# Four self attentions of a decoder: turns woven into the value products of the half batch behind, and no unread products

## The chip, the cores and the metric

The kernel runs on one core of one Trainium2 chip. The metric is the device time of one execution in microseconds (us). The names of the engines are PE (TensorE, the matrix products), PEld (its weight loads), DVE (VectorE), ACT (ScalarE), POOL (GpSimd) and SP (SyncE, which issues transfers).

## The reference

A decoder of four layers works on x, 16 batches of 100 tokens with 128 features. Each layer has a self attention, a cross attention and a feed forward block. The change is in the self attentions alone. They have 16 heads of 8 features each. Layer 0 (`sa0` in the kernel), cut to its core:

```python
scores = jnp.einsum('bhqd,bhkd->bhqk', q, k) * scale
scores = jnp.where(causal[None, None], scores, -jnp.inf)
probs = jax.nn.softmax(scores / TEMP, axis=-1)
probs = probs * gate
out = jnp.einsum('bhqk,bhkd->bhqd', probs, v)
return (out @ w_out.T + b_out) * 0.1
```

Layers 1 and 3 (`sa1`, `sa3`) have the same form: `sa1` has no biases and quantised weights, `sa3` has normed queries and keys and biases. Layer 2 (`sa2`) is a differential attention without a causal mask: two softmax maps for each head, values of 16 features, and a root-mean-square norm of each head's output before the last product.

```python
att = att1 - lam * att2
y = jnp.einsum('bhts,bhse->bhte', att, v)
y = y * jax.lax.rsqrt(jnp.mean(y * y, axis=-1, keepdims=True) + RMS_EPS) * subln_w
```

## The kernel before

Each engine has its own program, written out by hand, and the engines meet at semaphores. The order of each engine's work is the order of its loops in the code; no planner moves anything.

A self attention first makes queries and keys, splits them, and lays them out through DRAM. Then comes its main loop, which is what the change touches. The loop goes over units (`all_units`): 4 units in `sa0`, `sa1` and `sa3` (`nsm` = 1, 4 batches in a unit), 8 units in `sa2` (`nsm` = 2, 2 batches in a unit, two maps). A unit has 8 steps `k`, and a step is a half batch: 8 heads, in two groups `c` of 4. So the loops have 32, 32, 64 and 32 steps. For one half batch:

- PE: `scores(k)` makes the scores, 100 rows by 2 x 400 columns; in the causal layers each group is two products (the mask, then the scores). The results lie in banks 0 and 1 or 2 and 3, by the parity of `k`.
- DVE: `shift(k)` takes the row maxima (L1732) and subtracts them in place (L1733), and signals `shifted`.
- ACT: the exponential (L1188) of all 800 columns into `probs`, and signals `probs_ready`.
- PE: `turn(k)` transposes the 8 maps by products with the identity: 8 products of float32, which show as 16 records in the trace (L2652). Each group signals `turned`.
- ACT: two copies (L1200) bring the turned maps from PSUM into `probsT`, and signal `probsT_ready`.
- PE: `values(k)` multiplies the turned maps with the values: 8 products, 16 records (L2668), each with a full set of 100 x 100 weights and only 9 columns (17 in `sa2`). The last column counts the sum of the probabilities. Two half batches fill bank 7, and the second signals `o_full`.
- DVE: `normalise` divides by that sum (L1742, then L1745 or L1749) and gives bank 7 back with `o_free`. There is one such bank.

PE interleaves these over three half batches: in step k it does the four unread products, the turns of k, the scores of k + 2 and the value products of k - 1. The unread products (`unread`, L2640) are four products of 400 columns whose results nobody reads. Further, at set steps of a unit, PE makes the value rows of the next unit (`value_rows`, L2617 for the bias where there is one, and L2618), the transposes of the finished output of the unit before (`features`, L2681) and the last product (`project`, L2690). In `sa2`, DVE's `finish` and ACT's `root` work out the norm of the outputs (L1757 to L1764).

## Time and profile before

| | |
|---|---|
| median of 3 runs | 6178.4 us (6163.06 to 6204.71) |
| the profiled execution's own time | 6208.25 us |
| its span, first to last instruction | 6206.5 us |
| mean granted TensorE clock over the span | 0.818 of full speed |
| PE busy | 4731.2 us (76%) |
| DVE busy | 3437.1 us (55%) |
| ACT busy | 2441.8 us (39%) |
| main loops of the four self attentions, first to last row maxima | 161.2, 134.1, 345.4 and 161.9 us |

Busy shares are averages over stages with different limits, so a stage has to be read by itself. A full clock of 1.00 is 2.4 GHz, 0.50 is 1.2 GHz; a mean in between is a mixture of stretches at these two levels. A product of PE and the weight load of the next one overlap, and the end of a product is modelled, so the start of a record and the start of the next one tell more than a duration.

### The profile page before, as it was taken

The page shows a single profiled execution, that of the slowest core. Times are in us where ns is not written, and L with a number is a line of the kernel's source. Part 1 is how long each engine was busy: PE and PEld are TensorE (multiplying, and loading weights), DVE is VectorE, ACT ScalarE, POOL GpSimd, SP SyncE. Part 2 cuts the span into 40 slices and gives each one's busy share as a digit, 9 for nine tenths or more (in the row PEclk, how much of TensorE's full clock was granted, in tenths as well). Part 3 has the DMA queues.
Part 4 walks back from the last instruction along what each step waited for, and adds up shares of the span by engine and source line. Part 5 has one row for each costly group of instructions (what it writes and reads, how often), then busy time and mean ns, then how long its engine had stood idle before and what let it go on. Part 6 is the DMA issues. An engine that isn't in the chain of part 4 may idle for free. (4 is left out here: it accounts for less than half of the span.)

```text
span 6206.5 us, 84643 instructions
## 1 busy us (share of the span) xinstructions
PE 4731.2 (76%) x22582; PEld 3354.9 (54%) x22582; DVE 3437.1 (55%) x5067; ACT 2441.8 (39%) x3674; POOL 1999.7 (32%) x1091
## 2 busy tenths in 40 slices
PE   7999999999798866669878888888486444432698
PEld 6778778888544755348845555555274222221344
DVE  3444444444345422444556666664646999987444
ACT  2345555555222311123335555554123555540122
POOL 0055555555100000000036666664001555550000
PEclk7789999999799965687779999998677666655699
DMA  2100000000011312121111112110020000000011
GB/s 74 48 8 16 16 16 16 16 16 8 13 42 29 70 36 58 41 82 31 28 43 43 42 42 46 43 38 20 11 43 20 22 21 21 21 16 0 5 46 38
DMA packets 153375, 193.27 MB, mean 31 GB/s; under 512 B 91760, under 2 KB 136576, under 8 KB 152864
## 3 DMA queue, kind: packets, MB, share of 16 engines
q1 hardware_dynamic: 152992, 188.87, 12.5%
q8 instruction: 154, 2.52, 0.2%
q14 instruction: 229, 1.88, 0.1%
HBM read 134.07 MB, written 19.05 MB: 25 GB/s over the span
## 5 line engine op out<-in xcount | busy, mean ns | idle before, releaser
L1021 POOL TENSOR_TENSOR pexp_lo<-arena,pexp_hi 128x800 fp32r<-128x800 f32 x384 | 727.8, 1895 | 413.8 <-POOLq L1020 413.8
L976 POOL TENSOR_TENSOR pexp_lo<-arena,pexp_hi 128x800 fp32r<-128x800 f32 x384 | 628.4, 1636 | 515.6 <-POOLq L975 515.6
L1947 DVE TENSOR_REDUCE arena<-ps 128x1 f32<-128x482 f32 (+3 forms) x624 | 393.3, 657 | 404.1 <-DVEq L1925 388.9
L2092 DVE TENSOR_REDUCE arena<-ps 100x1 f32<-100x482 f32 (+1 forms) x768 | 476.6, 656 | 219.0 <-DVEq L2061 200.7
L1282 ACT ACTIVATE arena<-ps 128x800 f32<-128x800 f32 x384 | 322.3, 839 | 554.1 <-ACTq L1280 552.2
L1348 ACT ACTIVATE arena<-ps 128x800 f32<-128x800 f32 x384 | 321.7, 838 | 402.2 <-ACTq L1342 396.8
L2399 DVE MATCH_REPLACE8 arena<-arena 100x1444 f32<-100x1444 f32 x256 | 423.0, 1673 | 0.0
L3022 PE MATMUL ps<-kst,qs 96*100 96x482 f32 (+1 forms) x768 | 334.0, 436 | 116.4 <-PEq L2982 112.5
L1732 DVE TENSOR_REDUCE arena<-ps 100x8 f32<-100x800 f32 x160 | 158.7, 992 | 392.1 <-DVEq L1729 392.1
L3260 PE MATMUL ps<-arena,chunk 128*128 128x400 f32 x648 | 286.3, 524 | 72.6 <-PEq L3259 72.5
L2652 PE MATMUL ps<-w_const,arena 100*100 100x100 f32 x2560 | 311.2, 287 | 37.9 <-PEq L2648 37.9
L2652 PEld LDWEIGHTS ps<-w_const,arena 100*100 100x100 f32 x2560 | 309.6, 201 | 53.4 <-issue 42.9
L3164 PE MATMUL ps<-w_const,w_cross 100*128 100x100 f32 x192 | 43.2, 381 | 382.2 <-PEq L3161 382.2
L1283 ACT ACTIVATE pexp_hi<-ps 128x800 fp32r<-128x800 f32 x384 | 319.4, 832 | 0.0
L1349 ACT ACTIVATE pexp_hi<-ps 128x800 fp32r<-128x800 f32 x384 | 319.4, 832 | 0.0
L2389 DVE MAX8 arena<-arena 100x8 f32<-100x1444 f32 x192 | 311.5, 1677 | 0.0
L2489 DVE TENSOR_TENSOR arena<-ps,arena 128x400 f32<-128x400 f32 x256 | 147.0, 574 | 292.1 <-DVEq L2480 183.5
L1200 ACT ACTIVATE arena<-ps 100x400 f32<-100x400 f32 x320 | 160.5, 504 | 372.4 <-ACTq L1199 372.4
L1060 POOL TENSOR_TENSOR arena<-arena 100x1444 f32<-100x1444 f32 x64 | 207.8, 3246 | 285.9 <-POOLq L1059 285.9
L1524 ACT ACTIVATE arena<-ps 128x400 f32<-128x400 f32 x256 | 129.1, 504 | 423.6 <-ACTq L1521 423.4
L2914 PE MATMUL ps<-pexp_hi,ctxk_hi 128*97 128x400 f32 (+1 forms) x768 | 283.3, 369 | 15.1 <-PEq L2909 12.8
L921 POOL MEMSET k_diag<- 96x6400 f32 x4 | 21.7, 5428 | 833.2 <-POOLq L920 833.2
(358 smaller groups left out, 11004.8 us busy)
## 6 DMA issues: line engine op xcount, KB each, us to landing
ctxT<-in_ctxT SPq DMA_DIRECT2D x64, 541.5 KB
ctxk<-in_ctx SPq DMA_DIRECT2D x48, 528.0 KB
kst<-mid SPq DMA_DIRECT2D x128, 180.5 KB, 3.1
heads_dram<-arena SPq DMA_DIRECT2D x20, 800.0 KB
chunk<-in_ff_chunks SPq DMA_DIRECT2D x77, 193.0 KB, 2.4
arena<-gate_dram SPq DMA_DIRECT2D x64, 200.0 KB, 3.1
kst<-xn SPq DMA_DIRECT2D x64, 180.5 KB, 2.9
q_rows<-heads_dram SPq DMA_DIRECT2D x36, 200.0 KB
```

The lines of the kernel that those rows point to most:

```text
L976: own(nc.gpsimd.tensor_tensor(pexp_lo[p % 3][:, :, :], pexp[p % 3], pexp_hi[p % 3][:, :, :], ALU.subtract))
L1021: own(nc.gpsimd.tensor_tensor(pexp2_lo[p % 3][:, :, :], pexp2[p % 3], pexp2_hi[p % 3][:, :, :], ALU.subtract))
L1282: nc.scalar.activation(pexp[p % 3], of, ACT.Exp, scale=scale).then_inc(s.pexp_ready, 1)
L1283: own(nc.scalar.activation(pexp_hi[p % 3][:, :, :], of, ACT.Exp, scale=scale))
L1348: nc.scalar.activation(pexp2[p % 3], of, ACT.Exp, scale=scale).then_inc(s.pexp_ready, 1)
L1349: own(nc.scalar.activation(pexp2_hi[p % 3][:, :, :], of, ACT.Exp, scale=scale))
L1947: peak = nc.vector.tensor_reduce(mparts[0:at.stop - at.start, m, c:c + 1], bank(k, z - a, at.stop - at.start), AX.X, ALU.max)
L2092: peak = nc.vector.tensor_reduce(mparts2[:, h, c:c + 1], bank(k, z - a, S), AX.X, ALU.max)
L2389: nc.vector.max(tops[:, k, at], left[k]).then_inc(done[i], 1)
L2399: nc.vector.match_replace(left[k], tops[:, k, at], scores_sb[i] if r == 0 else left[k], TAKEN).then_inc(done[i], 1)
L2652: last = mm(bank(4 + c, S, S, j * S), probs[:, k % 2, at:at + S], ident[0:S, 0:S], start=True, stop=True)
L3022: ins = mm(bank(k, z - a, S), qs[par][0:C, g, S * (h % 4):S * (h % 4) + S], kst[0:C, g, a:z], start=True, stop=True)
```

## The change

On PE a step now has another order. It waits for the exponentials of k first, makes the scores of k + 2, and then goes through the 8 heads: one turn of half batch k, one value product of half batch k - 1, and so on. The waits for bank 7 (`o_free`) and for the values (`v_ready`) stand ahead of the first turn, and the wait for the turned maps of the half batch behind is taken group by group. The function `unread` and its calls are gone. In `sa2`, the two `features` move from steps 3 and 4 to 4 and 5 and `project` from 5 to 6; in the others they stay.

On ACT the exponential of k + 1 now comes before the copies of the turned maps of k; one exponential stands ahead of the loop.

On DVE, `finish` is cut in two: the squares and their sums stay at step 2, and the rest, which waits for ACT's root, is called at step `nsm` + 1 (3 in `sa2`, 2 in the others, where it only signals).

```diff
-    TURNS_AT = {1: (3,), 2: (3, 4)}
+    TURNS_AT = {1: (3,), 2: (4, 5)}
+    PROJECT_AT = {1: 5, 2: 6}
...
+            def exponential(k):
+                act.wait_ge(s.shifted, 1)
+                act.sem_inc(s.shifted, -1)
+                nc.scalar.activation(probs[:, k % 2, :].rearrange("p (c t) -> p c t", c=2),
+                                     ps[0:S, 2 * (k % 2):2 * (k % 2) + 2, 0:GT], ACT.Exp,
+                                     scale=float(cfg["scale"])).then_inc(s.probs_ready, 1)
...
             def unit(u, par, first=False, last=False):
                 for k in range(8):
...
+                    if k < 7 or not last:
+                        exponential((k + 1) % 8)
...
                     if not first and k == 2:
+                        squared_sums(1 - par)
+                    if not first and k == nsm + 1:
                         finish(1 - par)
...
-            def unread(n):
-
-                for i in range(n):
-                    mm(bank(4 + i % 2, GT, S), ident_bf[0:S, 0:S], causal_bf[:, :], start=True, stop=True)
-
-            def turn(k, first):
-                if not first:
-                    pe.wait_ge(s.probsT_ready, 2)
-                    pe.sem_inc(s.probsT_ready, -2)
-                unread(4)
-                pe.wait_ge(s.probs_ready, 1)
-                pe.sem_inc(s.probs_ready, -1)
...
+            def turns(k, behind, par):
+
+                if behind is not None:
+                    values_wait(behind)
                 for c in range(2):
+                    if behind is not None:
+                        pe.wait_ge(s.probsT_ready, 1)
+                        pe.sem_inc(s.probsT_ready, -1)
                     for j in range(4):
+                        at = c * GT + j * S
+                        ins = mm(bank(4 + c, S, S, j * S), probs[:, k % 2, at:at + S], ident[0:S, 0:S], start=True, stop=True)
+                        if j == 3:
+                            ins.then_inc(s.turned, 1)
+                        if behind is not None:
+                            value(behind, par, c, j)
...
             def unit(u, par, first=False, last=False):
                 for k in range(8):
-                    turn(k, first and k == 0)
+                    pe.wait_ge(s.probs_ready, 1)
+                    pe.sem_inc(s.probs_ready, -1)
                     if k < 6:
                         scores(k + 2, par)
                     elif not last:
                         scores(k - 6, 1 - par)
                     if k > 0:
-                        values(k - 1, par)
-                    elif not first:
-                        values(7, 1 - par)
+                        turns(k, k - 1, par)
+                    else:
+                        turns(0, None if first else 7, 1 - par)
```

The PE program at the second step (k = 1) of the first unit of `sa0`, before (unread products, turns, scores, value products, value rows):

```order
L2640 MATMUL ps<-causal_bf,ident_bf 100x400 [waits probsT_ready]
L2640 MATMUL ps<-causal_bf,ident_bf 100x400 x3
L2652 MATMUL ps<-w_const,arena 100x100 [waits probs_ready]
L2652 MATMUL ps<-w_const,arena 100x100 x7
L2633 MATMUL ps<-causal_bf,ident_bf 100x400
L2634 MATMUL ps<-k_diag_51,q_rows_49 100x400
L2633 MATMUL ps<-causal_bf,ident_bf 100x400
L2634 MATMUL ps<-k_diag_51,q_rows_49 100x400
L2668 MATMUL ps<-arena 100x9 [waits o_free,v_ready]
L2668 MATMUL ps<-arena 100x9 x7
```

The same step of the change, up to the turn that waits for the second group (L2645 and L2646 are the scores, L2678 a turn, L2663 a value product):

```order
L2645 MATMUL ps<-causal_bf,ident_bf 100x400 [waits probs_ready]
L2646 MATMUL ps<-k_diag_51,q_rows_49 100x400
L2645 MATMUL ps<-causal_bf,ident_bf 100x400
L2646 MATMUL ps<-k_diag_51,q_rows_49 100x400
L2678 MATMUL ps<-w_const,arena 100x100 [waits o_free,v_ready,probsT_ready]
L2663 MATMUL ps<-arena 100x9
L2678 MATMUL ps<-w_const,arena 100x100
L2663 MATMUL ps<-arena 100x9
L2678 MATMUL ps<-w_const,arena 100x100
L2663 MATMUL ps<-arena 100x9
L2678 MATMUL ps<-w_const,arena 100x100
L2663 MATMUL ps<-arena 100x9
```

The four products of 400 columns at the head are gone, the wait for `o_free` has moved from behind the turns and the scores to ahead of the turns, and each turn is followed by a value product.

The DVE program of `sa2` around steps 2 and 3 of a later unit, in the change (L1738 and L1739 are a shift, L1762 and L1763 the squares and their sums, L1771 to L1773 the rest of `finish`):

```order
L1748 RECIPROCAL arena<-ps 100x16 [waits dve_done,o_full]
L1755 TENSOR_TENSOR deviation<-ps,arena 100x256 [waits dve_done]
L1757 SCALAR_TENSOR_TENSOR arena<-deviation,col,arena 100x256 [waits dve_done]
L1762 TENSOR_TENSOR deviation<-arena 100x512 [waits dve_done]
L1763 TENSOR_REDUCE arena<-deviation 100x32 [waits dve_done]
L1738 TENSOR_REDUCE arena<-ps 100x8 [waits dve_done,scores]
L1739 TENSOR_TENSOR ps<-ps,arena 100x2x400 [waits dve_done]
L1771 RECIPROCAL arena<-arena 100x32 [waits dve_done,rms_root]
```

Before, the operation that waits for `rms_root` came directly behind the sums; now the shift of step 3 stands between them.

## Rows read from the trace of the kernel before

**Rows 1.** Windows over the four main loops: busy time of each engine and granted clock.
```profile
85.80:247.00 161.20, 159.97 (x1241) 146.41 (x1239) 71.81 (x94) 58.27 (x106) 0.00 (x0) 0.83 0.24 56
2048.70:2182.80 134.10, 131.95 (x1217) 123.01 (x1215) 70.57 (x92) 58.55 (x107) 0.00 (x0) 0.98 0.23 42
2760.30:3105.70 345.40, 312.55 (x2409) 288.60 (x2408) 177.23 (x243) 137.50 (x236) 0.00 (x0) 0.79 0.13 30
4532.50:4694.40 161.90, 159.74 (x1240) 146.46 (x1239) 71.83 (x94) 58.55 (x107) 0.00 (x0) 0.83 0.10 20
```
The columns are the stretch in us, its length, busy us (and instructions) of PE, PEld, DVE, ACT and POOL, then the granted clock, the DMA share and GB/s.

**Rows 2.** Timeline of PE, one step of `sa1`: start, us, operation, count.
```profile
2061.83 0.84 PE L2640 MATMUL ps<-causal_bf,ident_bf 100*100 100x400 bf16 x4
2062.51 1.57 PE L2652 MATMUL ps<-w_const,arena 100*100 100x100 f32 x16
2063.92 0.33 PE L2633 MATMUL ps<-causal_bf,ident_bf 100*100 100x400 bf16 x1
...
2064.62 1.50 PE L2668 MATMUL ps<-arena 100*100 100x9 f32 x16
2065.98 0.44 PE L2618 MATMUL ps<-w_sa,xn 128*100 128x128 f32 x2
```

**Rows 3.** Timeline of PE, one step of `sa2`.
```profile
2819.70 1.54 PE L2640 MATMUL ps<-causal_bf,ident_bf 100*100 100x400 bf16 x4
2821.03 2.87 PE L2652 MATMUL ps<-w_const,arena 100*100 100x100 f32 x16
2823.60 0.97 PE L2634 MATMUL ps<-k_diag,q_rows 96*100 96x400 f32 x2
2824.37 2.73 PE L2668 MATMUL ps<-arena 100*100 100x17 f32 x16
2826.94 0.57 PE L2681 MATMUL ps<-w_const,arena 100*128 100x100 f32 x2
```

**Rows 4.** Windows: granted clock of five stretches (the third number from the end).
```profile
2057.95:2182.80 124.85, 124.85 (x1185) 117.75 (x1183) 65.60 (x87) 54.42 (x101) 0.00 (x0) 1.00 0.22 41
2819.70:2839.50 19.80, 19.80 (x101) 18.22 (x100) 5.52 (x8) 4.63 (x9) 0.00 (x0) 0.50 0.10 25
...
2047.00:2051.05 4.05, 4.05 (x12) 2.61 (x12) 1.99 (x2) 0.00 (x0) 0.00 (x0) 0.50 0.54 106
...
98.70:102.00 3.30, 3.30 (x30) 2.96 (x30) 1.99 (x2) 1.29 (x3) 0.00 (x0) 1.00 0.00 0
102.10:105.40 3.30, 3.30 (x21) 3.13 (x19) 0.00 (x0) 0.71 (x2) 0.00 (x0) 0.50 0.00 0
```

**Rows 5.** Timeline of PE at a fall of the clock in `sa0`.
```profile
99.54 1.50 PE L2668 MATMUL ps<-arena 100*100 100x9 f32 x16
100.97 0.46 PE L2617 MATMUL ps<-w_sa,w_const 1*100 1x128 f32 x2
...
101.66 1.13 PE L2640 MATMUL ps<-causal_bf,ident_bf 100*100 100x400 bf16 x4
```

**Rows 6.** Timeline: the start of a loop, DVE, ACT, PE; the bracket is idle time before.
```profile
87.27 1.00 DVE L1733 TENSOR_TENSOR ps<-ps,arena 100x800 f32<-100x800 f32 x1 [0.51 <-DVEq L1691]
88.54 0.84 ACT L1188 ACTIVATE arena<-ps 100x800 f32<-100x800 f32 x1 [3.76 <-ACTq L1187]
89.52 2.96 PE L2652 MATMUL ps<-w_const,arena 100*100 100x100 f32 x16 [1.23 <-PEq L2648]
92.28 0.54 PE L2633 MATMUL ps<-causal_bf,ident_bf 100*100 100x400 bf16 x1
```

**Rows 7.** Timeline of DVE, `normalise` in `sa1`.
```profile
2092.97 0.26 DVE L1742 RECIPROCAL arena<-ps 100x16 f32<-100x16 f32 x1 [0.35 <-DVEq L1739]
2093.37 0.29 DVE L1745 TENSOR_TENSOR arena<-ps,arena 100x128 f32<-100x128 f32 x1
```

**Rows 8.** Timeline of PE, the last product of a unit of `sa2`, and what follows.
```profile
2834.54 1.68 PE L2690 MATMUL ps<-arena,w_sa 128*128 128x200 f32 x4
2836.02 1.54 PE L2640 MATMUL ps<-causal_bf,ident_bf 100*100 100x400 bf16 x4
```

**Rows 9.** Waits of PE in the loop of `sa2`: total us, times, longest.
```profile
PE ps L2652 <- PEq L2648: 32.4, 8, 4.9
```

More of the change, by code:

```diff
@@ L1204, in self_attention @@
                 value_rows(0, i, i)
+            exponential(0)
             all_units(nsm, unit)
@@ L1759, in finish @@
                     dve.sem_inc(s.rms_sum, 1)
+            def finish(par):
+                if cfg.get("diff"):
+                    y3 = y_tok[:, par, :].rearrange("p (h w) -> p h w", w=16)
                     dve.wait_ge(s.rms_root, 1)
@@ L1797, in self_attention @@
             normalise(3, 1)
+            squared_sums(1)
             finish(1)
@@ L2635, in scores, with values_wait @@
                 last.then_inc(s.scores, 1)
-            def unread(n):
-                for i in range(n):
-                    mm(bank(4 + i % 2, GT, S), ident_bf[0:S, 0:S], causal_bf[:, :], start=True, stop=True)
-            def turn(k, first):
-                if not first:
-                    pe.wait_ge(s.probsT_ready, 2)
-                    pe.sem_inc(s.probsT_ready, -2)
-                unread(4)
-                pe.wait_ge(s.probs_ready, 1)
-                pe.sem_inc(s.probs_ready, -1)
-                for c in range(2):
-                    for j in range(4):
-                        at = c * GT + j * S
-                        last = mm(bank(4 + c, S, S, j * S), probs[:, k % 2, at:at + S], ident[0:S, 0:S], start=True, stop=True)
-                    last.then_inc(s.turned, 1)
-            def values(k, par):
+            def values_wait(k):
                 slot, half = k // 2, k % 2
-                i, sm = slot // nsm, slot % nsm
                 if half == 0:
@@ L2660, in values, with value @@
                     pe.sem_inc(s.o_free, -1)
[L2661 removed]
+                if half == 0 and slot % nsm == 0:
                     pe.wait_ge(s.v_ready, 1)
                     pe.sem_inc(s.v_ready, -1)
+            def value(k, par, c, j):
+                slot, half = k // 2, k % 2
+                h = 8 * half + 4 * c + j
+                at = 16 * (vw + 1) * (slot // nsm) + h * (vw + 1)
+                ins = mm(bank(7, vw + 1, S, h * (vw + 1)), probsT[:, k % 2, c * GT + j * S:c * GT + j * S + S],
+                         vaug[:, par, at:at + vw + 1], start=True, stop=True)
+                if h == 15:
+                    ins.then_inc(s.o_full, 1)
+            def turns(k, behind, par):
+                if behind is not None:
+                    values_wait(behind)
                 for c in range(2):
+                    if behind is not None:
+                        pe.wait_ge(s.probsT_ready, 1)
+                        pe.sem_inc(s.probsT_ready, -1)
                     for j in range(4):
[L2666 to L2671 removed]
+                        at = c * GT + j * S
[4 more added lines that the diff above has]
+                            value(behind, par, c, j)
             def features(par, c):
@@ L2708, in unit @@
                         features(1 - par, k - TURNS_AT[nsm][0])
-                    if not first and k == 5:
+                    if not first and k == PROJECT_AT[nsm]:
                         project()
@@ L2718, in self_attention @@
             pe.sem_inc(s.probsT_ready, -2)
-            values(7, 1)
+            values_wait(7)
+            for c in range(2):
+                for j in range(4):
+                    value(7, 1, c, j)
             for c in range(nsm):
```

15 lines of the change are left out of this document (1 added, 14 removed).

## The prediction, made before the change was run

> **What bounds the kernel now.** I read the windows over the four loops first, since the change touches nothing else: 161.2, 134.1, 345.4 and 161.9 us, 802.6 together, 13% of the span [rows 1]. In the three causal loops PE is busy for all but 1 to 2 us, DVE for under 72 us and ACT for under 59, so PE sets their pace; in `sa2` PE is idle for 33 us, nearly all in one wait per unit for exponentials [rows 1, 9]. The same column shows the second thing: the granted clock is 0.98 in `sa1` but 0.83, 0.79 and 0.83 in the others [rows 1]. `sa0` and `sa1` do nearly the same work and differ by 27 us. So PE's work and PE's clock are the two quantities.
>
> A step at the full level, by differences of starts [rows 2]: unread 0.68, turns 1.41, scores 0.70, values 1.36, value rows about 0.3, thus 4.15 without value rows. A step at the half level in `sa2` [rows 3], which lies in a stretch at 0.50 [rows 4]: unread 1.33, turns 2.57, scores 0.77, values 2.57, features 0.37. Everything doubles, also the values, though they have only 17 columns: their pace of 0.09 and 0.16 us for a record is that of the turns, so both are paced by weights, and these follow the clock.
>
> **What makes the clock rise and fall.** The loop of `sa1` starts at 0.50 and rises behind 4.05 us that PE filled without a gap with scores and unread products, all 400 columns wide [rows 4]. In `sa0` the clock fell, with no idle gap, behind a stretch with the scores, the 16 thin value records and the one-row bias products [rows 4, 5]; then unread products, turns and scores follow each other for over 4 us and it can rise again. In `sa1`, without such bias products, it held 1.00 for 124.85 us on end [rows 4]. So thin products let the clock fall, and only a long unbroken run of wide ones lifts it. At the half level the old order has such a run in every step: 1.33 + 2.57 + scores (0.77, and 1.4 in the causal layers), 4.7 to 5.3 us.
>
> **The change, part by part.**
>
> *Unread products gone.* Each step loses 0.68 us at full level or 1.33 at half. That is on the path wherever PE is the bound.
>
> *Turns woven with values.* The counts stay. At equal clock the woven part takes the sum of its parts: 2.77 us at full, 5.14 at half. Since every record, wide or thin, is paced by its 100 x 100 weights, I see no gain from hiding a load behind a turn, nor a loss. But the wide run is broken: behind each turn comes a thin product. At the half level the longest wide run in a steady step is now the scores, 0.8 us in `sa2` and 1.4 in the others; with `project` in front it is 1.5 more [rows 8]. Only step 0 of the first unit has no values behind: there scores and turns run for 1.34 + 2.7 us [rows 6]. All four loops start at the half level, as before, and two causal loops have one-row products right behind that run. So the clock has one good chance to rise at the start of each loop and a weak one at each `project`, where it had one in every step.
>
> *The wait for bank 7.* It stands ahead of the turns. Every second step, `normalise` of the slot just filled must be through. Its chain: from the end of the last value record, about 0.15 us behind the next start, 0.14 to the next engine (the exponential ends at 89.38, PE starts at 89.52) [rows 6], reciprocal and product 0.69 from first start to last end [rows 7], 0.27 from DVE's end over its own wait to the engine that waits (88.27 to 88.54) [rows 6]: 1.25 us. At full, scores cover 0.70 of it, so PE idles about 0.55 us in each odd step. Behind the waiting turn are all turns and values of the step. At half, in the causal loops, 1.4 us of scores cover it; in `sa2` 0.77 do not, and about 0.6 is left (its `normalise` is a little longer). Before, unread products, turns and scores covered it fully, so that is a new cost, and its idle time comes directly ahead of the thin, woven stretch: the worst place for a clock that is at the full level.
>
> *Exponential ahead of the copies.* It takes the exponential off the chain from one step to the next. Scores are two steps ahead, and DVE (2.1 us a step) and ACT (about 2) have slack at either level, so I count it as nothing in the causal loops. Its cover is PE's own 3.5 us or more a step.
>
> *`finish` in two, `features` and `project` a step later.* In `sa2` this takes away the wait of up to 4.9 us in each unit, 32.4 us in all [rows 9]: a root, two table loads and DVE's wait for it no longer hold back the exponential that PE wants next. At half, with steps of 5.9 us or more, I take all of it as hidden. At full, about 4 us a unit would be left, since the chain is nearly as long.
>
> **The sum.** First all at the half level. A causal step is 2.57 + 2.57 + scores of 1.44 = 6.58 us; 31 of them are 204. `sa1`: value rows 12 x 0.42, `project` 3 x 1.5, features 2 us, 215 against 134, +81. `sa0`, `sa3`: value rows with bias, 0.69 at full [rows 5], about 1.3 at half, 12 of them: 226 against 161 and 162, +65 each. `sa2`: 63 x 5.91 = 372, the bank wait 31 x 0.6 = 19, value rows 14 x 0.8, features 14 x 0.37, `project` 7 x 1.5: 419 against 345, +74. Together +285 us.
>
> Then what the full level gives back. There a causal step is 2.77 + 0.70 + 0.55/2 = 3.75 us, so a step saves 2.8, with side work 3.0. I estimate that `sa1` gets it at the start three times in four, `sa0` and `sa3` once in four, a `project` lifts it one time in five, and that it lasts about ten steps, until an idle bank wait and the woven stretch push it down. That is some 12 steps of 32 in `sa1` and 6 each in `sa0` and `sa3`: 24 or 25 steps, -75 us. In `sa2`, whose bank wait at full is longest, nearly nothing. The sum is +285 - 75 = +210 us. The profiled execution took 6208.25 us, 1.75 around its span and 0.5% above the median of 6178.4; counted from the median the forecast is 6178 + 210, about **6390 us**, 3.4% slower.
>
> **Two rules weighed.** The value records at the half level are at 0.16 us [rows 3] against 0.09 at full [rows 2]. The Trainium skill, "TensorE: Matmul & The Clock Gate", section "LDWEIGHTS", gives the load a fixed rate by columns (P / 1.2 ns) that knows no clock level. By it the 16 value records at half would stay near 1.4 us, the steps 1.2 us shorter, and the all-half sum would be about +100 instead of +285; the trace speaks against it, and I go by the rows.
>
> **The rivals.**
>
> *A: the full level holds, and the kernel gets faster.* In the new order PE has no long idle gap in the steady loops, only 0.55 us in each second step. If the clock asks only for PE to be occupied, it rises at the start and stays. Then: causal steps 3.75 us; `sa1` 123 (-11), `sa0` and `sa3` 128 (-33, -34). `sa2`: steps of 1.35 + 0.42 + 1.36 = 3.13, bank waits 31 x 1.0, side work 15, chain 28: 271 (-74). Together -152, **6026 us**. It decides from the point where a woven stretch at the half level is enough to lift the clock. For it: in `sa1` PE held 1.00 with values a third of the step. Against it: the falls in `sa0` with PE busy throughout [rows 4, 5]. Chance 0.11. The Trainium skill, "TensorE: Matmul & The Clock Gate", section "Why this matters for your kernels", has such a rule: avoid drops by leaving no long PE-idle gaps between bursts. By it this rival is the outcome; here the trace shows a fall without a gap, so I give it little.
>
> *B: the causal loops get up and mostly stay, `sa2` does not.* With 85% of the 93 causal steps at full: +285 - 79 x 3.0 = +48, **6226 us**, the same within what can be told. It needs a bank wait well under 0.5 us and an easy rise. Chance 0.08.
>
> *C: the level is full for half or more of the causal steps.* +285 - 56 x 3.0 = +117, **6295 us**. Chance 0.15.
>
> *D: nothing rises at all.* +285, **6463 us**, with a little more if the waits for turned maps also show. It is the upper end of the forecast's own case, which with it has 0.66.
>
> A version in which the change does not do what it says is excluded by the order shown: the unread products are gone.
>
> **The numbers.** A measurement of this kernel tells about 1% (62 us) from no change. Faster is A, 0.11; same is B, 0.08 and a little of C, 0.09; slower is the rest, 0.80. The range leaves out A and reaches from between B and C to D with the 0.5% by which an execution can lie above the median: 6250 to 6490.
>
> **What would show it.** Granted clock in the four loops: forecast 0.5 to 0.7, in `sa2` near 0.5; by A over 0.95. Woven part of a step: 5.1 to 5.3 us at half, 2.8 at full. PE's idle time ahead of the first turn of odd steps: 0.5 to 0.6 at full, none at half in the causal loops, 0.6 in `sa2`. The wait for exponentials once a unit in `sa2` gone. If woven records at half go at 0.09 us where they are thin, the step of the weights fails; if the clock rises from woven stretches, the step of the clock does, and the time is that of A.

## The result: 4.7% slower, and the profile after

The changed kernel took 6470.6 us (median of 4 runs, 6449.29 to 6479.48) against 6174.5 for the kernel before on the same chip. The ratio is 1.047, with a 95% interval of 1.042 to 1.051. The profiled execution took 6469.07 us with a span of 6467.2. The forecast was 6390 us in a range of 6250 to 6490.

The same windows as in [rows 1], now over the four loops of the changed kernel:

```profile
84.40:300.30 215.90, 213.11 (x1101) 196.44 (x1099) 71.81 (x94) 57.60 (x104) 0.00 (x0) 0.50 0.18 42
2100.90:2291.20 190.30, 184.99 (x1077) 171.90 (x1076) 70.50 (x92) 56.50 (x105) 0.00 (x0) 0.56 0.17 30
2857.80:3291.50 433.70, 388.89 (x2142) 365.63 (x2141) 177.16 (x242) 136.36 (x233) 0.00 (x0) 0.51 0.10 24
4729.30:4946.10 216.80, 213.09 (x1101) 196.41 (x1099) 71.82 (x94) 57.81 (x105) 0.00 (x0) 0.50 0.07 14
```

The loops grew by 54.7, 56.2, 88.3 and 54.9 us, 254 in all, of 260.7 us by which the span grew. PE has fewer records (1101 against 1241 in `sa0`) and is busy for longer (213 against 160 us). The clock says why: 0.50, 0.56, 0.51 and 0.50, from 0.83, 0.98, 0.79 and 0.83. `sa0` and `sa3` never left the half level (below, the half level is a granted clock of 0.50 and the full level one of 1.00; a wide product streams 100 columns or more, a thin one 9 or 17; the bias product has one row and counts as neither; a run is a stretch in which PE makes wide products without a break).

PE at the first steps of `sa0`, up to the first pairs of turn and value product:

```profile
88.84 0.54 PE L2645 MATMUL ps<-causal_bf,ident_bf 100*100 100x400 bf16 x1
88.91 0.80 PE L2646 MATMUL ps<-k_diag,q_rows 96*100 96x400 f32 x1
89.50 2.87 PE L2678 MATMUL ps<-w_const,arena 100*100 100x100 f32 x16
92.31 0.74 PE L2629 MATMUL ps<-w_sa,w_const 1*100 1x128 f32 x2
...
95.43 0.63 PE L2678 MATMUL ps<-w_const,arena 100*100 100x100 f32 x2
95.86 0.39 PE L2663 MATMUL ps<-arena 100*100 100x9 f32 x2
96.10 0.63 PE L2678 MATMUL ps<-w_const,arena 100*100 100x100 f32 x2
```

From 88.17, where the scores of step 0 begin, to 92.31 PE runs wide products, 4.1 us; then one-row products; and from 94.86 on every turn has a thin product behind it. Two turn records and two value records take 0.67 us (95.43 to 96.10), 0.167 us each: the value records at half run at the pace of the turns, as [rows 3] showed it.

Two loops got up: `sa1` twice, and `sa2` once in its first unit, for 10.2 us. Windows of the clock, three in `sa1` in order, then its second high stretch, then that of `sa2`:

```profile
2104.00:2111.30 7.30, 5.78 (x27) 5.28 (x28) 3.33 (x4) 4.11 (x7) 0.00 (x0) 0.50 0.38 48
2111.40:2128.40 17.00, 15.87 (x162) 14.94 (x160) 10.22 (x14) 7.28 (x14) 0.00 (x0) 1.00 0.01 2
2128.50:2247.80 119.30, 119.20 (x630) 111.56 (x630) 38.12 (x51) 31.64 (x61) 0.00 (x0) 0.50 0.23 42
2247.90:2254.70 6.80, 6.36 (x68) 5.98 (x67) 4.53 (x6) 2.41 (x5) 0.00 (x0) 1.00 0.01 2
...
2865.70:2875.90 10.20, 9.21 (x94) 8.71 (x94) 6.60 (x8) 4.89 (x10) 0.00 (x0) 1.00 0.04 11
```

`sa1` held 1.00 for 17 us and then stood at 0.50 for 119 us, in which PE was idle for 0.1 us. Ahead of its first rise the same work stood as at the start of `sa0`, but without the one-row products:

```profile
2106.86 2.87 PE L2678 MATMUL ps<-w_const,arena 100*100 100x100 f32 x16
2109.53 0.63 PE L2630 MATMUL ps<-w_sa,xn 128*100 128x128 f32 x2
2109.95 0.54 PE L2645 MATMUL ps<-causal_bf,ident_bf 100*100 100x400 bf16 x1
...
2111.29 0.37 PE L2678 MATMUL ps<-w_const,arena 100*100 100x100 f32 x2
```

With the scores that begin at 2105.52 this is a run of 5.8 us. The timeline of PE at the last steps of the high stretch:

```profile
2119.44 0.39 PE L2678 MATMUL ps<-w_const,arena 100*100 100x100 f32 x2 [0.44 <-PEq L2675]
...
2122.26 0.35 PE L2645 MATMUL ps<-causal_bf,ident_bf 100*100 100x400 bf16 x1
...
2122.99 0.34 PE L2678 MATMUL ps<-w_const,arena 100*100 100x100 f32 x2
...
2125.75 0.35 PE L2645 MATMUL ps<-causal_bf,ident_bf 100*100 100x400 bf16 x1
...
2127.34 0.39 PE L2678 MATMUL ps<-w_const,arena 100*100 100x100 f32 x2 [0.69 <-PEq L2675]
```

A step without the wait takes 3.49 us (2122.26 to 2125.75), with a woven part of 2.76. In the next, a step with the wait for bank 7, PE idles 0.69 us ahead of the turns; an earlier step with that wait, at 2119.44, shows 0.44, since value rows stand ahead of it. The clock fell 1.1 us behind the 0.69.

In `sa2` the wait of [rows 9] is gone, but another has come. DVE and PE around step 7 of a unit:

```profile
3069.77 0.36 DVE L1785 TENSOR_TENSOR x<-ps,x 128x200 f32<-128x200 f32 x1 [10.94 <-DVEq L1778]
3070.48 0.99 DVE L1738 TENSOR_REDUCE arena<-ps 100x8 f32<-100x800 f32 x1 [0.35 <-DVEq L1735]
3071.62 1.00 DVE L1739 TENSOR_TENSOR ps<-ps,arena 100x800 f32<-100x800 f32 x1
3072.97 0.26 DVE L1748 RECIPROCAL arena<-ps 100x16 f32<-100x16 f32 x1 [0.35 <-DVEq L1745]
3073.38 0.42 DVE L1751 TENSOR_TENSOR arena<-ps,arena 100x256 f32<-100x256 f32 x1
```

```profile
3067.94 1.68 PE L2701 MATMUL ps<-arena,w_sa 128*128 128x200 f32 x4
3069.15 1.14 PE L2646 MATMUL ps<-k_diag,q_rows 96*100 96x400 f32 x2
3074.60 0.63 PE L2678 MATMUL ps<-w_const,arena 100*100 100x100 f32 x2 [4.31 <-PEq L2675]
```

DVE waits 10.9 us at its `update` (L1785) for the product that PE makes at the end of step 6 (L2701). Behind that wait are the next shift and the `normalise` that gives bank 7 back, and PE cannot go on without it: 4.0 to 4.3 us of idle PE, six times in the loop, 24 us. All PE waits ahead of turns in this loop come to 41.9 us, against 32.4 before:

```profile
PE ps L2678 <- PEq L2675: 41.9, 24, 4.3
```

### The profile page after: what moved, and what is told of

It reads as the page before. It is cut to its first block and busy times, and to the rows that moved or that the text cites. A ratio compares the mean times of both kernels' runs of the same rounds, so it can differ in the third digit from the quotient of the medians.

```text
span 6467.2 us, 83519 instructions
## 1 busy us (share of the span) xinstructions
PE 4963.3 (77%) x21942; PEld 3593.5 (56%) x21942; DVE 3436.1 (53%) x5067; ACT 2439.3 (38%) x3674; POOL 1999.4 (31%) x1091
## 5 line engine op out<-in xcount | busy, mean ns | idle before, releaser
L2678 PE MATMUL ps<-w_const,arena 100*100 100x100 f32 x2560 | 772.8, 408 | 50.7 <-PEq L2675 50.0
L2678 PEld LDWEIGHTS ps<-w_const,arena 100*100 100x100 f32 x2560 | 572.9, 279 | 89.6 <-issue 80.3
L2663 PEld LDWEIGHTS ps<-arena 100*100 100x100 f32 x2560 | 563.1, 280 | 2.6 <-issue 2.6
L2663 PE MATMUL ps<-arena 100*100 100x9 f32 (+1 forms) x2560 | 493.4, 271 | 2.4 <-PEq L2730 2.4
L1738 DVE TENSOR_REDUCE arena<-ps 100x8 f32<-100x800 f32 x160 | 158.7, 992 | 400.6 <-DVEq L1735 400.6
```

What stands on the lines that cost most here:

```text
L2663: ins = mm(bank(7, vw + 1, S, h * (vw + 1)), probsT[:, k % 2, c * GT + j * S:c * GT + j * S + S], vaug[:, par, at:at + vw + 1], start=True ...
L2678: ins = mm(bank(4 + c, S, S, j * S), probs[:, k % 2, at:at + S], ident[0:S, 0:S], start=True, stop=True)
```

## The experiments

All ratios are to the kernel before on the same chip, with 95% intervals. The loops are given in the order `sa0`, `sa1`, `sa2`, `sa3`, from the profiled execution, from the first row maxima to the last; the ends of the windows shown are rounded to 0.1 us. Only the lines of an edit that matter are shown: `...` marks what is left out, and where an edit calls `unread` in the changed kernel it also defines it again, as it was in the kernel before.

**The unread products back, in the woven order** (`woven_unread`).

```diff
                 if behind is not None:
-                    values_wait(behind)
+                    pe.wait_ge(s.probsT_ready, 2)
+                    pe.sem_inc(s.probsT_ready, -2)
+                unread(4)
+                if behind is not None:
+                    values_wait(behind)
                 for c in range(2):
-                    if behind is not None:
-                        pe.wait_ge(s.probsT_ready, 1)
-                        pe.sem_inc(s.probsT_ready, -1)
                     for j in range(4):
```

> The changed kernel with four unread products of 400 columns put back, behind the scores and ahead of the woven turns and values, in every step; ahead of them PE waits for both turned groups, behind them for bank 7. Theory (only a long unbroken run of wide products lifts the clock): in a steady step at the half level the run is scores + unread = 2.7 us, too short to lift; only step 0, whose turns have no values behind, gives scores + unread + turns = 5.3 us and lifts each loop at its start. Where nothing then makes it fall (sa1: bank wait covered by the unread products, no one-row products) it stays: sa1 near 134 us at a clock of 0.95 or more. sa0 and sa3 may fall at one-row products and cannot come back (7.9 us a step at half); sa2 falls at its idle gap at step 7 and then goes at 7.2 us a step, some 460 to 490 us. Whole kernel 6330 to 6560. Rival (unread products hold the clock wherever they stand): all four loops near those of the kernel before, 6150 to 6190.

Measured: 6343.7 us, 1.026 (1.022 to 1.031); loops 194.2, 135.7, 457.5 and 191.7 us.

```profile
84.30:278.40 194.10, 191.53 (x1219) 169.40 (x1218) 71.81 (x94) 56.85 (x104) 0.00 (x0) 0.68 0.19 46
2079.00:2214.70 135.70, 132.21 (x1195) 119.49 (x1194) 70.54 (x92) 56.43 (x105) 0.00 (x0) 0.96 0.24 41
2778.10:3235.60 457.50, 430.09 (x2388) 384.60 (x2387) 177.24 (x243) 136.36 (x233) 0.00 (x0) 0.56 0.10 23
```

The rival is out: the unread products do not hold the clock wherever they stand. `sa1` shows that the woven order can be carried at the full level (0.96): it was lifted once and then had no wait of PE. `sa0` and `sa2` show that after a fall it does not come back soon, though every step has a run of 2.7 us (2.1 in `sa2`): `sa0` fell at 131.1, right behind one-row products, and stood at half for 116 us with PE always busy. It came back 31 us before its end, behind a `project`. `sa3` went against the expectation. It was not lifted at its start, rose once for 3.4 us behind a run of 3.2 us (value rows, scores and unread products), rose again behind a `project`, and then stayed at the full level to its end through five groups of one-row products:

```profile
4663.90:4786.80 122.90, 119.41 (x587) 104.73 (x586) 36.28 (x46) 29.50 (x53) 0.00 (x0) 0.51 0.11 22
4786.80:4855.70 68.90, 68.90 (x634) 62.14 (x632) 35.61 (x50) 27.64 (x52) 0.00 (x0) 1.00 0.04 6
```

So the expectation was too strict in two points: a woven loop can come back, and at the full level one-row products did not always bring the clock down.

**The unread products alone taken out of the kernel before** (`old_no_unread`).

```diff
-                unread(4)
+                unread(0)
```

> The kernel before, unread products alone taken out. Theory: the unbroken wide run at the half level shrinks from 5.3 to 4.0 us in the causal loops and from 4.7 to 3.4 in sa2, so it lifts the clock less often: sa1 rises within some steps and then holds, 110 to 125 us; sa0 and sa3 fall at their one-row products and stay down longer, 160 to 200; sa2 370 to 430, mostly at half. Whole kernel 6170 to 6300. Rival (the weaving alone spoils the clock, unread products are pure cost): each of 160 steps gains at least 0.68 us, 6060 or less.

Measured: 6269.1 us, 1.011 (1.004 to 1.017); loops 159.4, 146.7, 349.7 and 196.2 us at clocks of 0.72, 0.77, 0.62 and 0.57. The rival is out: 160 steps without unread products gained nothing. `sa1` was worse than forecast: it fell in its third unit, stayed low for some six steps (44 us), and fell again near its end. `sa2` came out 20 us below its range.

**Only the weaving undone** (`unwoven`): scores, eight turns, the wait for bank 7, eight values; no unread products; ACT and DVE as changed.

```diff
                 if behind is not None:
-                    values_wait(behind)
+                    pe.wait_ge(s.probsT_ready, 2)
+                    pe.sem_inc(s.probsT_ready, -2)
                 for c in range(2):
...
                         if j == 3:
                             ins.then_inc(s.turned, 1)
-                        if behind is not None:
+                if behind is not None:
+                    values_wait(behind)
+                    for c in range(2):
+                        for j in range(4):
                             value(behind, par, c, j)
```

> The changed kernel with one thing undone: all eight turns first, then the wait for bank 7, then all eight value products; still no unread products, ACT and DVE as changed. Theory: run of scores + turns 4.0 us at half (3.4 in sa2), so the causal loops come out like those of the old order without unread products (sa1 110 to 125, sa0 and sa3 160 to 200), and sa2 360 to 430. Whole kernel 6150 to 6320. Rival (ACT's and DVE's new order is what costs): it stays within 30 us of the changed kernel, 6440 or more.

Measured: 6230.5 us, 1.009 (1.005 to 1.013); loops 176.0, 114.5, 345.5 and 174.1 us.

```profile
84.30:260.30 176.00, 173.43 (x1108) 162.38 (x1107) 71.84 (x95) 58.71 (x104) 0.00 (x0) 0.63 0.22 52
2078.70:2193.20 114.50, 111.01 (x1084) 106.71 (x1083) 70.57 (x93) 59.50 (x105) 0.00 (x0) 0.95 0.27 49
2771.40:3116.90 345.50, 318.80 (x2147) 308.19 (x2146) 177.23 (x243) 137.74 (x233) 0.00 (x0) 0.65 0.13 30
```

The same products in another order: PE's counts are within 7 of those of the changed kernel, and PE's busy time falls from 213 to 173 us in `sa0` and from 185 to 111 in `sa1`. 240 of the 296 us are in the order of turns and values. The edit also puts the wait for bank 7 behind the turns, but that is not where the time went: PE was idle for 2.8 us of `sa0` in the changed kernel and for 2.6 here. `sa2`, at 345.5, came out below its range of 360 to 430. And `sa1` at 114.5 us is 20 us faster than before: in this order the unread products are pure cost there (133.2 with them in the next run, 113.5 to 113.9 in five runs without them below), while in the old order `sa1` was slower without them (146.7).

**The unread products back in the unwoven order** (`unwoven_unread`).

```diff
                 if behind is not None:
                     pe.wait_ge(s.probsT_ready, 2)
                     pe.sem_inc(s.probsT_ready, -2)
+                unread(4)
                 for c in range(2):
```

> The changed kernel with turns and values apart again (scores, four unread products, eight turns, the wait for bank 7, eight values) and the unread products back: PE's work and its runs are those of the kernel before, ACT's and DVE's order is the changed one. Theory (the clock follows the runs): run at half 5.3 us, causal loops as before within 6 us (161, 134, 162). sa2 loses the exponential wait but keeps the idle time at step 7: 325 to 350. Whole kernel 6150 to 6185. Rival (ACT's and DVE's new order costs in itself): 6220 or more.

Measured: 6192.1 us, 1.001 (0.997 to 1.004); loops 156.6, 133.2, 347.5 and 151.1 us.

```profile
84.10:240.70 156.60, 154.03 (x1220) 139.56 (x1219) 71.84 (x94) 58.72 (x104) 0.00 (x0) 0.85 0.24 58
2716.40:3063.90 347.50, 312.13 (x2388) 286.13 (x2387) 177.24 (x243) 137.14 (x233) 0.00 (x0) 0.81 0.12 30
```

PE's runs are those of before (only the scores now stand ahead of the unread products), and the time is that of before: ACT's and DVE's new order costs nothing in the causal loops (5, 1 and 11 us are won), and in `sa2` the old wait has been exchanged for another. PE is idle for 35 us there, against 33 before. The rival is out, though the median lies 7 us above the expected range.

**Every loop lifted at its start, nothing else** (`lift_start`): 24 unread products ahead of the loop of the changed kernel.

```diff
             scores(0, 0)
             scores(1, 0)
+            unread(24)
             all_units(nsm, unit)
```

> The changed kernel with 24 unread products in front of each loop (8 us at the half level), none inside: every loop starts at the full level. Theory (the woven order cannot keep the full level, since each second step has 0.4 to 0.7 us of idle PE ahead of a thin stretch, and cannot win it back): each loop runs some 4 to 12 steps at 3.5 to 4.2 us and then stays at half to its end, clocks 0.50 to 0.70; sa0 and sa3 180 to 210 us, sa2 400 to 430; the kernel 6380 to 6470. Rival (the woven order only lacks a start): clocks over 0.9, causal loops 120 to 135, sa2 270, the kernel 6030 to 6080.

Measured: 6475.8 us, 1.045 (1.039 to 1.051); loops 201.8, 188.3, 435.6 and 199.3 us. In `sa0`:

```profile
86.00:109.80 23.80, 23.10 (x204) 20.56 (x203) 13.95 (x18) 11.22 (x20) 0.00 (x0) 1.00 0.01 3
109.90:285.80 175.90, 175.71 (x917) 162.81 (x916) 56.27 (x77) 46.09 (x84) 0.00 (x0) 0.50 0.21 49
```

The loop starts at 1.00, takes seven steps at 2.8 to 4.2 us, falls, and then PE works for 176 us with 0.2 us of idle time at 0.50. So a missing start is not the cause. In all four loops, what came right ahead of the first fall is a wait for bank 7:

```profile
109.61 0.45 PE L2683 MATMUL ps<-w_const,arena 100*100 100x100 f32 x2 [0.70 <-PEq L2680]
2158.45 0.39 PE L2683 MATMUL ps<-w_const,arena 100*100 100x100 f32 x2 [0.70 <-PEq L2680]
2904.11 0.39 PE L2683 MATMUL ps<-w_const,arena 100*100 100x100 f32 x2 [1.03 <-PEq L2680]
4792.13 0.39 PE L2683 MATMUL ps<-w_const,arena 100*100 100x100 f32 x2 [0.69 <-PEq L2680]
```

The clock fell at 109.8, 2161.2, 2905.3 and 4792.9, 0.2 to 2.8 us behind. The two falls of the changed kernel at 2128.4 and 2875.9 came 1.1 and 2.0 us behind waits of 0.69 and 0.99. Three short stretches later in these loops, behind a `project`, ended behind waits of 0.44 or none. The woven `sa1` of `woven_unread`, in which PE never waits in its high stretch, did not fall. A run that changes the wait alone was not made. The loops are 32 us shorter together, with the 24 products, 4.7 us in `sa0`, included. The kernel as a whole came out 6 us above the expected range, since the other stages took 52 us more in the profiled execution, 46 of them between `sa0` and `sa1`, where nothing is changed; the cause of that was not sought. `sa2`, at 435.6, is above its 400 to 430.

**The bias products left out of the kernel before** (`old_no_bias_rows`); the values of `sa0` and `sa3` then lack their bias.

```diff
-                if cfg["bias"]:
-                    mm(bank(6, 16 * vw, S), W("const", "ones")[0:1, 0:S], W(wst, "bv")[:, 0:16 * vw], start=True, stop=False)
-                mm(bank(6, 16 * vw, S), xn[:, per * u + i, :], wv[:, 0:16 * vw], start=not cfg["bias"],
+                mm(bank(6, 16 * vw, S), xn[:, per * u + i, :], wv[:, 0:16 * vw], start=True,
```

> The kernel before without the one-row product of the value bias in sa0 and sa3, so their values lack the bias. Theory (the falls in sa0 and sa3 come from these one-row products next to the value products): both loops go like sa1, 131 to 137 us at a clock of 0.95 or more, from 161 and 162; the kernel 50 to 60 us faster, 6115 to 6130. Rival (their falls have another cause, as the gate or the start at the half level): only the products' own 12 x 0.4 to 0.7 us go, 153 to 157 us each, the kernel 6160 or more.

Measured: 6141.4 us, 0.992 (0.990 to 0.995); loops 133.7, 134.0, 344.9 and 134.0 us.

```profile
83.60:217.30 133.70, 132.47 (x1217) 123.68 (x1216) 71.87 (x95) 58.33 (x106) 0.00 (x0) 0.97 0.30 69
4502.80:4636.80 134.00, 131.76 (x1216) 123.17 (x1215) 71.86 (x94) 58.54 (x107) 0.00 (x0) 0.98 0.13 24
```

There are 24 records (12 products) fewer, and each loop loses 28 us, where the products themselves, at 0.4 to 0.7 us, would make 5 to 8. The falls in `sa0` and `sa3` went with the one-row products: PE is busy in them, and the clock falls. That it takes their place beside the value products is not shown by this run. The kernel gained 47 us, where 50 to 60 were expected, and its median lies 11 us above the range.

**The update of `sa2` moved** (`update_late`).

```diff
                     if not first and k in (0, 2):
                         normalise(k // 2 + 2, 1 - par)
+                    if nsm == 2 and k == 0 and u > 1:
+                        update(u - 2)
...
-                    if not first and k == 7:
+                    if nsm == 1 and not first and k == 7:
                         update(u - 1)
...
             all_units(nsm, unit)
+            if nsm == 2:
+                update(4 * nsm - 2)
```

> The changed kernel; in sa2 alone DVE adds a unit's projected output to x one step later, behind the normalise of step 0 of the next unit, instead of at step 7 ahead of it. Theory (in the changed kernel DVE waits at step 7 for the product that PE makes at the end of step 6, and the normalise that gives bank 7 back to PE is queued behind it, about 4 us of idle PE a unit): sa2 loses 25 to 30 us of its 434, the kernel 6435 to 6450. Rival (the idle time comes from the exponentials, not from bank 7): sa2 within 5 us of 434, no change.

Measured: 6458.8 us, 1.045 (1.040 to 1.050), within the error of the changed kernel's 1.047; loops 216.0, 207.7, 415.5 and 217.1 us. `sa2` fell by 18 us where 25 to 30 were expected, and the median lies 9 us above its range. A unit fell from 58.6 to 54.4 us (its last two steps from 13.8 + 3.7 to 6.3 + 7.4), which makes 25 in six units, but the first unit did not get up this time as it had in the changed kernel and took 8 back. PE's waits ahead of turns went from 41.9 us to 17.4:

```profile
PE ps L2682 <- PEq L2679: 17.4, 18, 2.3
```

The long wait is bank 7's, as read. `sa1` did not get up at all: 207.7 us is what the loop costs wholly at the half level. This was chance: PE made the same records at the same distances as at the start of `sa1` in the changed kernel, 5.77 us of them (2116.12 to 2121.89 here, 2105.52 to 2111.29 there), with 3.49 us of idle time ahead in both, and the clock rose there and not here.

**Versions put together from these.** `mixed` takes the unwoven order, four unread products in `sa2`, two in `sa0` and `sa3`, none in `sa1`, the late update, and ACT's `root` ahead of the exponential of step 3; in `sa0` and `sa3` the value rows of steps 1, 2 and 6 stand right behind the scores.

```diff
-                    if k < 7 or not last:
-                        exponential((k + 1) % 8)
                     if not first and k == 2 and cfg.get("diff"):
                         root()
+                    if k < 7 or not last:
+                        exponential((k + 1) % 8)
```

> A version put together from what was seen: turns and values apart, unread products only where a run needs them (none in sa1, two a step in sa0 and sa3, four in sa2), in sa0 and sa3 the value rows of steps 1, 2 and 6 ahead of the unread products, so that one-row and thin products are not neighbours, in sa2 the update late and ACT's root ahead of the exponential of step 3. Theory: sa1 115 us; sa0 and sa3 135 to 155 at a clock of 0.85 or more; sa2 290 to 320; the kernel 6060 to 6110. Rival (two unread products and early rows don't keep sa0 and sa3 up, or the early rows make PE wait for bank 6): they stay at 160 or more, and the kernel at 6120 or more.

Measured: 6102.0 us, 0.985 (0.980 to 0.990); loops 169.9, 113.5, 275.7 and 174.0 us. `sa2` fell by 70 us to 275.7 at a clock of 0.93, 14 below its range: with the waits gone PE has no gap of some us in a unit any more, and stays up but for 10 us. `sa0` and `sa3` went the rival's way, though the kernel stayed within its range.

`mixed_four`: four unread products there instead of two.

```diff
-                unread(4 if nsm == 2 else 2 if cfg["bias"] else 0)
+                unread(4 if nsm == 2 or cfg["bias"] else 0)
```

> The mixed version with four unread products a step in sa0 and sa3 instead of two. Theory (there the run at half was 4.7 us in steps without value rows and lifted too seldom; with four it is 5.3, and value rows apart from the value products let it stay): sa0 and sa3 140 to 152 us from 170 and 174, at a clock of 0.88 or more; sa1 and sa2 as in the mixed version; the kernel 6045 to 6070. Rival (the early value rows are what keeps them low, since they cut the run): 160 or more each, the kernel 6085 or more.

Measured: 6103.7 us, 0.988 (0.985 to 0.991); loops 159.3, 113.7, 275.8 and 169.6 us. Missed, and the kernel is 34 us above its range: hardly better. The rival that the early value rows cut the run is nearly met (159.3 and 169.6 against 160 or more).

`mixed_two`: two unread products in `sa2` instead of four.

```diff
-                unread(4 if nsm == 2 or cfg["bias"] else 0)
+                unread(2 if nsm == 2 else 4 if cfg["bias"] else 0)
```

> As mixed_four, but two unread products a step in sa2 instead of four. Theory (sa2 now stands at a clock of 0.93 and has few idle gaps; two products less save up to 0.34 us a step, 21 us in all, but the run at half shrinks from 4.7 to 4.1 us, so after its idle gap at the end of a unit it stays low longer): sa2 260 to 320, likeliest a little slower than its 276. Rival (unread products are no longer needed once the waits are gone): 250 to 260.

Measured: 6168.6 us, 0.998 (0.995 to 1.000); loops 165.5, 113.6, 330.7 and 160.1 us. Two products fewer in each step of `sa2` cost 55 us, by a clock of 0.70 in place of 0.93, 11 more than the expected range allowed. PE had fewer records and was busy for longer. `sa2` of `mixed_four`, then of `mixed_two`:

```profile
2698.20:2973.90 275.70, 266.39 (x2388) 246.24 (x2387) 177.13 (x242) 138.93 (x233) 0.00 (x0) 0.93 0.16 38
2710.70:3041.40 330.70, 320.34 (x2267) 301.80 (x2266) 177.18 (x242) 139.21 (x233) 0.00 (x0) 0.70 0.13 31
```

`mixed_late`: the value rows of `sa0` and `sa3` back behind the value products.

```diff
-                    early = k > 0 and cfg["bias"]
-                    if early and k in VALUES_AT[nsm] and not last:
-                        value_rows(u + 1, VALUES_AT[nsm].index(k))
...
-                    if not early and k in VALUES_AT[nsm] and not last:
+                    if k in VALUES_AT[nsm] and not last:
```

> The mixed version with four unread products in sa0, sa3 and sa2, none in sa1, and with the value rows back behind the value products. Theory (early value rows cut the wide run in three of eight steps and that cost more lifts than it saved falls): sa0 and sa3 as in the unwoven kernel with unread products, 151 to 160 us; sa1 113, sa2 276; the kernel 6070 to 6100. Rival (where the rows stand makes no difference): sa0 and sa3 160 to 170 as in the version with four, 6100 or more.

Measured: 6108.1 us, 0.987 (0.985 to 0.990); loops 156.6, 113.9, 266.4 and 157.5 us. The two loops came out as expected; the kernel's median was 8 us above the range.

`mixed_behind`: in `sa0` and `sa3` the four unread products stand between the value products and the value rows.

```diff
-                if behind is not None:
+                if behind is not None and not cfg["bias"]:
                     pe.wait_ge(s.probsT_ready, 2)
                     pe.sem_inc(s.probsT_ready, -2)
-                unread(4 if nsm == 2 or cfg["bias"] else 0)
+                unread(4 if nsm == 2 else 0)
...
                             value(behind, par, c, j)
+                if cfg["bias"]:
+                    pe.wait_ge(s.probsT_ready, 2)
+                    pe.sem_inc(s.probsT_ready, -2)
+                    unread(4)
```

> As mixed_late, but in sa0 and sa3 the four unread products stand behind the value products, between them and the value rows with their one-row products, instead of ahead of the turns. Theory (falls come from value products and one-row products as direct neighbours; here four wide products part them, and in steps without value rows unread + scores + turns still run 5.3 us unbroken): once up they stay, clock 0.90 or more, sa0 and sa3 135 to 145 us; the kernel 6030 to 6065. Rival (it is the share of thin and one-row products in a step that counts, not their being neighbours): 151 us or more each, no gain over mixed_late.

Measured: 6087.5 us, 0.985 (0.982 to 0.988); loops 145.4, 113.5, 270.0 and 151.3 us.

```profile
83.50:229.00 145.50, 142.17 (x1221) 128.09 (x1220) 71.84 (x95) 60.56 (x104) 0.00 (x0) 0.93 0.26 62
2011.30:2124.80 113.50, 110.02 (x1084) 105.79 (x1083) 70.56 (x93) 59.41 (x105) 0.00 (x0) 0.96 0.29 49
2701.80:2971.80 270.00, 260.82 (x2388) 241.27 (x2387) 177.16 (x242) 138.97 (x233) 0.00 (x0) 0.96 0.16 38
4405.80:4557.10 151.30, 147.05 (x1221) 131.23 (x1220) 71.84 (x95) 60.76 (x105) 0.00 (x0) 0.89 0.11 21
```

The kernel is 22 us above its range, and the expectation was met in part: the same products in the same number as in `mixed_late`, and 11 and 6 us less, but `sa0` lies at the upper end of 135 to 145 and `sa3` came out at the rival's 151. In `sa3` the loop stayed low for its first five steps (to 4439.7) and held the full level from then on, so the late rise accounts for the rest. There is one profiled execution of each kernel, and the same records have cost 17 us more in one than in another (`sa1` in `update_late`), so 11 and 6 us show the mechanism only weakly. This version is faster than both kernels, by 1.5% against the one before. It is not told apart from the other mixed ones at 0.985 to 0.988. The loops lost 122 us together and the median 99; outside the loops the profiled executions of all these kernels differ by some tens of us.

## Why the prediction was right, step by step

**PE bounds the loops, and two quantities set its time.** Right: PE busy was 213 of 216 us in `sa0` after the change. In `sa2` it was 389 of 434, and the rest was waits.

**Everything on PE follows the clock, the value records too.** Right: 0.167 us a record at half against 0.086 at full (2.76 us for 32 records), thin or wide. The Trainium skill's rate for weight loads that knows no level ("TensorE: Matmul & The Clock Gate", section "LDWEIGHTS"), by which the sum would have been about +100, gives 0.083 us for 100 columns as an estimate; it agrees with the rows at full and disagrees with those at half.

**Weaving costs nothing at equal clock.** Right: 2.76 us woven at full against a forecast of 2.77.

**Only a long unbroken run of wide products lifts.** Right in what it forecast, and shown by experiment in this: undoing the weaving took 240 us off with the same products; lifting the loops by hand did not help; unread products beside a woven part mostly did not bring a loop back. The rises in woven loops away from their starts, eight in three runs, came behind the longest runs of those loops, 2.8 to 4.1 us: a `project` with the scores (2244.89 to 2247.70 in the changed kernel, the rise at 2247.9), the same with unread products, or twice value rows, scores and unread products. Stated as a rule it is too strong, all the same. The run need not be enough: [rows 3, 4] have 4.7 us of it in each step and 19.8 us at 0.50, and the same 5.77 us lifted `sa1` in the changed kernel and not in `update_late`. And no run here tells whether it must be unbroken, or only so many wide products close together; the experiments leave both. Rival A, by which an occupied PE is enough, is out: PE worked for 176 us with 0.2 us of idle time at 0.50. The rule of the Trainium skill that gave this rival ("TensorE: Matmul & The Clock Gate", section "Why this matters for your kernels": leave no long idle gaps) is thus not enough here; the rows show a loop without gaps that does not rise.

**How often it rises.** This term was mis-sized. I gave 24 of 96 causal steps to the full level, -75 us. In the profiled execution it was 17 us, some five steps, and a stretch of 6.8 us behind a `project`, all in `sa1`, worth 17 us against the 207.7 of a loop wholly at half. `sa0` and `sa3` did not rise once, and in `sa2` 10.2 us at full gave back 8. Of nine `project`s in the causal loops one lifted the clock, where I had taken one in five, and for two steps, not ten. At the start of `sa0` the one-row products stand in the middle of the long run (92.31), and `sa1` has none; that this decides was not tested in the woven order. The likeliest case should have been D, and that `sa1` rose at its start was chance.

**The causal loops wholly at half.** 226 us forecast for `sa0`, 216 measured, since the first three steps, without values behind and with the pipeline filling, take 2.8, 2.6 and 5.4 us and not 6.6.

**The wait for bank 7.** 0.55 us forecast at the full level, 0.69 measured, and 0.44 where value rows fill part of it. That it comes at the worst place fits: all six high stretches that began at or near the start of a woven loop without unread products, in the changed kernel and in `lift_start`, ended 0.2 to 2.8 us behind such a wait of 0.69 to 1.03. None was seen at half in the causal loops, as forecast.

**`finish`, `features` and `project` a step later, hidden at half.** This step failed. I followed what the moves release and not what stands behind them on DVE: with `project` at step 6, DVE's `update` at step 7 has to wait for it, and `normalise` is queued behind. It cost 4.0 to 4.3 us in each of six units and made PE's waits ahead of turns 41.9 us, where 19 had been forecast and 32.4 had been there before; `update_late` showed the place: 17.4 us of waits, and 4.2 us less a unit. `sa2` was forecast at +74 and came at +88.

**The sum.** +285 was forecast for all at half. The three causal loops were 27 us cheaper (216, 208 and 217 against 226, 215 and 226), the waits in `sa2` 23 dearer, and the full level gave back 25 and not 75: +256, and the loops gave +254. The first two errors cancel nearly by luck; the +210 was low because of the 75. The span grew by 260.7 and the median by 296: the profiled execution of the kernel before, at 6208.25 us, lay 34 above its median of 6174.5 and above all four of its timed runs, and that of the changed kernel, at 6469.07, at its median.

What is left open: whether the waits alone make a woven loop fall, and why `sa1` fell in `old_no_unread` and not in `unwoven`, with the same run of 4.0 us. The traces have one difference: in `old_no_unread` PE waited 0.39 us ahead of the value products at 2108.89 and 0.25 at 2167.75, and the clock fell at 2111.5 and 2169.5; in `unwoven` PE never waited in the high stretch of `sa1`. An earlier wait of 0.25, at 2100.30, was followed by no fall, so this is a hint and not a cause shown.

## What to carry to other kernels

Before taking out or reordering PE work, find the stretches at the half level and ask what lifted the clock at the end of each; if it was a run of wide products, that run may be worth more than its own time, and breaking it up can cost more than removing it (247 us in the four loops here, against 49 for taking the unread products out of the old order). Write down what stood ahead of each rise and each fall; they need not be the same thing. One execution is not enough for this: the same records lifted a loop once and once not. And when a product is moved a step later, read on in the queue of the engine that takes it: the wait moves too, and what stands behind it decides.

## What the runs showed of the hardware that was not expected

- The same products at the same engine, in two orders, took 213 and 173 us of PE in one loop and 185 and 111 in another.
- Without 24 records of one-row products a loop got 28 us faster and its mean clock went from 0.83 to 0.97, while PE was busy for all but 1.3 us in both. In `sa3` of `woven_unread`, though, five groups of them stood in 69 us at 1.00.
- The half level held for 216 us on end with PE idle for under 3 us.
- Both levels lasted: in `sa0` of `woven_unread` PE was busy without a gap for 38 us at 1.00, for 116 at 0.50 and for 31 at 1.00 again, in nearly the same steps.
- The same 5.77 us of the same records, behind the same idle time, were followed by a rise in one execution and by none in another.
